# A gated attention stage: one projection step in every unit, maxima over eleven units, rank operations one at a time, masked products in other units

## The reference, cut to what matters

```python
ss = sigmoid(x @ Ws).reshape(b, t, H, E)          # H = 8 heads, E = 5 experts, DH = 64
sd = sigmoid(x @ Wd).reshape(b, t, H, E)
ms, md = topk_mask(ss, 3), topk_mask(sd, 3)       # the 3 best of 5 experts
q = einsum('bthed,bthe->bhtd', q5, sd * md)       # q5, k5, v5: x projected per head and expert
k = einsum('bthed,bthe->bhtd', k5, ss * ms)
v = einsum('bthed,bthe->bhtd', v5, ss * ms)
out = softmax(q k^T * DH**-0.5) v
y = einsum('bthem,bthe->btm', (out @ Wo).reshape(b, t, H, E, DIM), md)
```

## Time and profile before

| quantity | value |
|---|---|
| median of three runs | 4450.3 us |
| the profiled execution | 4442.77 us, span 4441.0 us |
| PE, DVE, POOL, ACT busy over the span | 87%, 73%, 66%, 43% |
| mean granted PE clock | 0.944 of full |
| gated stage | 1233.3 to 2619.7 us of the span |
| its pairs 0 to 13 | 1330.8 to 2459.4 us |
| pair 14, pair 15 with the ending | 60.7 us, 99.6 us |

### The profile page before, as it was taken

One profiled execution on the slowest core, in us unless ns is written; L12 is line 12 of the kernel. 1 busy time (PEld: TensorE's weight loads), 2 busy tenths in 40 slices (PEclk: granted clock), 3 DMA queues, 4 the chain that ended last, 5 costly groups with the idle time before them and its releaser, 6 DMA issues. The chain is left out here.

```text
span 4441.0 us, 63434 instructions
## 1 busy us (share of the span) xinstructions
PE 3881.5 (87%) x22554; PEld 2209.9 (50%) x22554; DVE 3243.7 (73%) x5656; ACT 1923.2 (43%) x3478; POOL 2937.1 (66%) x2164
## 2 busy tenths in 40 slices
PE   5998998999868889889899847999999999999964
PEld 3555555555445555555555423555455445545523
DVE  3786877868577787777876627888788788878826
ACT  1443443444345455455455312444344444434423
POOL 0776775757626777877887833777677677767740
PEclk6999999999979999999999957999999999999987
DMA  3000000000020000100000021122212221212111
GB/s 53 14 14 14 24 14 24 18 6 6 1 75 27 19 28 27 37 19 28 32 28 10 6 62 25 29 38 35 39 29 40 32 40 29 42 24 41 19 53 33
DMA packets 98041, 125.90 MB, mean 28 GB/s; under 512 B 28896, under 2 KB 76448, under 8 KB 97728
## 3 DMA queue, kind: packets, MB, share of 16 engines
q1 hardware_dynamic: 97728, 121.86, 12.5%
HBM read 103.69 MB, written 18.12 MB: 27 GB/s over the span
## 5 line engine op out<-in xcount | busy, mean ns | idle before, releaser
L776 POOL TENSOR_TENSOR s_psum_p<-s_psum_p,s_prob 128x1024 f32<-128x1024 f32 (+3 forms) x640 | 1335.6, 2087 | 388.3 <-ACT s_prob L511 338.3
L511 ACT ACTIVATE s_prob<-s_sT 128x1024 f32<-128x1024 f32 (+2 forms) x896 | 791.6, 931 | 877.2 <-DVE s_sT L658 495.1
L412 PE MATMUL s_pv<-s_prob,s_vp 128*64 128x512 f32 (+3 forms) x3584 | 797.7, 566 | 3.9 <-POOL s_prob L761 3.9
L614 DVE CUSTOM_DVE_ANT_0 s_mx<-s_mx,s_strip 128x512 f32<-128x512 f32 x640 | 429.6, 712 | 177.2 <-PE s_mx L371 174.7
L1670 POOL TENSOR_TENSOR s_psum_p<-s_psum_p,s_prob 128x1024 f32<-128x1024 f32 x192 | 462.1, 2407 | 104.7 <-ACT s_prob L1393 102.6
L1393 ACT ACTIVATE s_prob<-s_sT 128x1024 f32<-128x1024 f32 x256 | 262.4, 1025 | 581.9 <-PE s_sT L1257 581.9
L371 PE MATMUL s_mx<-s_bh,s_ah 64*128 64x512 f32 (+3 forms) x1792 | 412.1, 455 | 110.3 <-DVE s_bm L604 48.3
L663 DVE RECIPROCAL s_recip<-s_recip 128x128 f32<-128x128 f32 x512 | 452.4, 921 | 35.2 <-ACT s_recip L459 35.2
L776 POOL TENSOR_TENSOR s_psum_p<-s_prob 128x1024 f32<-128x1024 f32 (+1 forms) x128 | 288.0, 2250 | 236.2 <-ACT s_prob L511 233.5
L604 DVE TENSOR_REDUCE s_bm<-s_mx 128x8 f32<-128x1024 f32 (+3 forms) x384 | 367.4, 957 | 54.6 <-PE s_mx L371 45.7
L371 PEld LDWEIGHTS s_mx<-s_bh,s_ah 64*128 64x128 f32 x1792 | 171.9, 188 | 466.6 <-issue 192.1
(11 more groups left out here) (251 smaller groups left out, 7395.6 us busy)
## 6 DMA issues: line engine op xcount, KB each, us to landing
s_strip<-bias_rows SPq DMA_DIRECT2D x256, 144.0 KB, 5.7
s_wr<-gated_weights SPq DMA_DIRECT2D x32, 960.0 KB, 4.8
s_near<-bias_rows SPq DMA_DIRECT2D x256, 48.0 KB, 2.0
x<-s_x SPq DMA_DIRECT2D x12, 512.0 KB, 3.2
s_x<-x SPq DMA_DIRECT2D x8, 512.0 KB, 5.1
gated_weights<-s_side_hi SPq DMA_DIRECT2D x8, 480.0 KB, 2.6
gated_weights<-s_side_lo SPq DMA_DIRECT2D x8, 480.0 KB, 2.9
s_x<-in_L_attn_x_dram SPq DMA_DIRECT2D x4, 512.0 KB, 4.3
```

Source lines behind the costliest of these rows:

```text
L412: last = mm(pv[heads(hd), lo:CH], vp[:, g % 2, j, heads(hd)], prob[:, k % PR, hd, lo:CH], start=j == 0, stop=end)
L511: nc.scalar.activation(prob[:, k % PR, :, lo:CH], sT[:, k % 2, :, lo:CH], ACT.Exp, scale=st.scale).then_inc(exp_done, 1)
L614: last = nc.vector.tensor_tensor_reduce(out=mx[:, hd, :], in0=mx[:, hd, :], in1=strip[:, g % 2, hd, first:first + CH], scale=1.0, scalar=N ...
L776: nc.gpsimd.tensor_tensor(out[:, :, lo:CH], src, p[:, :, lo:CH], ALU.add)\
```

## The change

Only the gated stage's schedule and what follows from it. Projections: one in each of the 16 units, so that every one borrows. Maxima: one in units 4 to 9, two in 10 to 14. `mt` moves to unit 15 and, on PE and DVE, ahead of that unit's projection. Masked products of tokens 0 to 3 move to units 0 to 3 of the next pair; those of the last pair go to the head of `ending`. `gx` and `gl` move to units 12 to 15 of pairs 0, 3, 7; the ranks' sixteen operations become single jobs in units 0 to 9 of pairs 1, 4, 8. `xs` and `ln` are moved. Items take half 0 of queries and keys first, then half 1, and wait only for the projection steps that they read.

```diff
-TOPS, TOPC = E0 + 1, 8 + 3 * (E0 - 1)
+TOPS, TOPC = 4 + 3 * (E0 - 1), 8 + 3 * (E0 - 1)
...
-        self.mx_steps = [0] * 4 + [1] * 6 + [2, 2, 3, 3, 0, 0]
-        self.pj_steps = [2] * 4 + [1] * 8 + [0] * 4
+        self.mt_unit = 15
+        self.mx_steps = [0] * 4 + [1] * 6 + [2] * 5 + [0]
+        self.pj_steps = [1] * self.U
...
-            for i in range(4, NB):
-                out[3 + i].append(("zp", g - 1, i))
+            for i in range(NB):
+                out[i if i < 4 else 3 + i].append(("zp", g - 1, i))
...
-        for i in range(4):
-            out[12 + i].append(("zp", g, i))
...
-            for u, job in ((6, ("gx", gated, 0)), (7, ("gx", gated, 1)), (8, ("gl", gated, 0)),
-                           (9, ("gl", gated, 1)), (10, ("top", gated, 0)), (11, ("top", gated, 1)),
-                           (14, ("top", gated, 2))):
+            for u, job in ((12, ("gx", gated, 0)), (13, ("gx", gated, 1)), (14, ("gl", gated, 0)),
+                           (15, ("gl", gated, 1))):
...
-            for k, u in enumerate((8, 9, 11)):
-                out[u].append(("top", ranked, 3 + k))
+            for n, u in enumerate((0, 1, 2, 3, 4, 4, 5, 5, 6, 6, 7, 7, 7, 8, 9, 9)):
+                out[u].append(("top", ranked, n))
...
-        if p == 1 and b + 1 < B:
-            for k in range(2):
-                out[12 + k].append(("xs", b + 1, k))
-        for n, (of, u) in enumerate(((1, 13), (1, 14), (1, 15), (2, 2), (2, 3), (2, 6), (2, 7))):
+        if b + 1 < B and p in (1, 2):
+            out[13 if p == 1 else 0].append(("xs", b + 1, p - 1))
+        for n, (of, u) in enumerate(((1, 15), (1, 15), (2, 4), (2, 5), (2, 6), (2, 6), (2, 9))):
...
+        ending = [("zp", GP - 1, i) for i in range(4)] + ending
...
-                    pe.wait_ge(p_done, 2 * 2 * NB * (of + 1))
+                    pe.wait_ge(p_done, 2 * step(of, NB + 4 * (k // 2) + 4)[0])
...
+                if ("mt", g + 1) in todo:
+                    m_transpose(g + 1)
                 for n, t in enumerate(steps):
                     project(t[1], t[2], k if n == 0 else None)
...
-                if ("mt", g + 1) in todo:
-                    m_transpose(g + 1)
```

More of the change, by code:

```diff
@@ L1122, in misc_job @@
                 if kind == "item":
-                    pe.wait_ge(p_done, 2 * 2 * NB * (of + 1))
+                    pe.wait_ge(p_done, 2 * step(of, NB + 4 * (k // 2) + 4)[0])
                     for n in range(4):
                         last = nc.tensor.transpose(misc[:, n * P:(n + 1) * P],
-                                                   qkv[:, of % 3, 4 * (k % 2) + n, k // 2, :], cst.ident[:, :])
+                                                   qkv[:, of % 3, 4 * (k // 2) + n, k % 2, :], cst.ident[:, :])
                     last.then_inc(ab_full, 1)
@@ L1175, in project @@
                 m, hd, i = step(g, n)
-                if n == 0:
-                    pe.wait_ge(xl_done, 2 * (g // NP) + 2)
+                if n in (0, 4):
+                    pe.wait_ge(xl_done, 2 * (g // NP) + 1 + n // 4)
                 if n % NB == 0:
@@ L1324, in misc_job @@
                         act.wait_ge(st_full, (of - 1) * U)
-                    dst = ah if k < 2 else bh
-                    copy(dst[:, of % 2, half(k % 2)], misc[:, :]).then_inc(hi_done, 1)
+                    dst = bh if k % 2 else ah
+                    copy(dst[:, of % 2, half(k // 2)], misc[:, :]).then_inc(hi_done, 1)
                 elif kind == "gx":
@@ L1363, in x_hi @@
                 if b > 0:
-                    act.wait_ge(px_full, 2 * NB * NP * b)
+                    act.wait_ge(px_full, 2 * NB * NP * b - 4 * (1 - c))
                 copy(xh[:, half(c)], xT[:, half(c)]).then_inc(xh_done, 1)
@@ L1444, in misc_job @@
                 if kind == "item":
-                    hi, lo = (ah, al) if k < 2 else (bh, bl)
-                    cols = half(k % 2)
+                    hi, lo = (bh, bl) if k % 2 else (ah, al)
+                    cols = half(k // 2)
                     dve.wait_ge(hi_done, 4 * of + k + 1)
@@ L1512, in x_lo, with top_experts @@
                 tt(xl[:, half(c)], xT[:, half(c)], f32(xh[:, half(c)]), ALU.subtract).then_inc(xl_done, 1)
-            def top_experts(b, k):
+            def top_experts(b, n):
                 gates, kept = gate[:, b % 2, :, :], keep[:, :, :]
-                at = TOPC * b + E0 + 3 * (k - 1)
-                if k == 0:
+                k, part = divmod(n + 2, 3)
+                if n == 0:
                     dve.wait_ge(sig_done, 2 * b + 2)
@@ L1521, in top_experts @@
                         nc.vector.memset(kept[:, e, :], float(E0 - 1 - e)).then_inc(top_step, 1)
-                elif k < E0:
+                    return
+                dve.wait_ge(top_step, TOPC * b + E0 + n - 1)
+                if k < E0:
                     later, earlier, won = slice(k, E0), slice(0, E0 - k), beats[:, 0:E0 - k, :]
[L1524 to L1529, removed]
-                else:
[L1531 to L1535, removed]
+                    if part == 0:
+                        ins = tt(won, gates[:, earlier, :], gates[:, later, :], ALU.is_ge)
+                    elif part == 1:
+                        ins = tt(kept[:, later, :], kept[:, later, :], won, ALU.add)
+                    else:
+                        ins = tt(kept[:, earlier, :], kept[:, earlier, :], won, ALU.subtract)
+                elif part == 0:
+                    ins = nc.vector.tensor_scalar(kept, kept, float(TOP) - 0.5, None, ALU.is_lt)
+                elif part == 1:
+                    ins = tt(gates, gates, kept, ALU.mult)
+                else:
                     if b >= 2:
                         dve.wait_ge(share_done, 2 * NP * (b - 1))
-                    nc.vector.tensor_copy(
+                    ins = nc.vector.tensor_copy(
                         keep_d[:, b % 2, :, :, :],
-                        kept.rearrange("p e (i s h) -> p e i s h", i=NB, s=2)[:, :, :, 1, :])\
-                        .then_inc(top_step, 1)
+                        kept.rearrange("p e (i s h) -> p e i s h", i=NB, s=2)[:, :, :, 1, :])
+                ins.then_inc(top_step, 1)
+                if n == TOPS - 1:
                     dve.wait_ge(top_step, TOPC * (b + 1))
@@ L1624, in _ @@
                     maxima(t[1], t[2], second(todo, t, k))
+                if ("mt", g + 1) in todo:
+                    max_rows(g + 1)
                 for n, t in enumerate(steps):
@@ L1632, in _ @@
                             head_maxima(t[1])
-                    elif t[0] == "mt":
-                        max_rows(t[1])
                     elif t[0] == "ln":
```

## The result

The changed kernel takes 4466.4 us (median of six runs, 4462.3 to 4467.2) against 4449.8 for the kernel before in its six (4441.8 to 4451.1): ratio 1.0037, 95% interval [1.0025, 1.0049]. It is slower by 17 us, where the prediction has 4472 against 4450.3, slower by 22. The profiled execution has a span of 4460.7 us, 19.7 over that of before.

A forecast was written before the change was run, and what follows sets the result against it. PE bounds units 0 to 3, a chain through the borrowed half of sT units like 6, DVE the last four. Terms +52 +5 -24 -6 -3 +3 = +27 on 4442.8 give 4470, taken as 4472 us; range 4447 to 4503.

The forecast's parts named there:

- The chain through the borrowed half: Scores, projection, DVE scalings, scores, once a unit: units 0 to 3 -3.2 us, 12 to 15 +6.9; +52 over fourteen pairs.
- The upper bound: Upper limit of the cost in the changed units: 0.3 us more a unit for unseen waits, +4.9 a pair, +69.
- Masked products: Four products moved into units 0 to 3 meet POOL's additions: +5 us, bounds 0 and +24.
- The term of 0.6 in nine ordinary pairs: Only the worst meeting of product and addition, in unit 2, reaches the chain: +0.6 us a pair, +5 in all.
- The upper bound's 1.7 a pair: Upper limit for masked products: half a 4.28 us less DVE's spare time, in every pair, 14 x 1.7 = +24.
- Ranks: Groups cost about 39 us; single operations leave 5 in each of pairs 1, 4, 8: -24, bounds -36 and -10.
- Output projection: Its y and gt now lie in units with slack: 3 x (3.1 - 1.2) = -6 us.
- xs, ln: They move between units of about equal slack: -3 us, bounds -5 and +5.
- The end: Pair 14 and after: four masked products reach into pair 14, four more into the ending: +3 us, bounds -3 and +10.
- Rival A: A wash: same mechanism, borrowed waits cost less (+2.5 us a pair), ranks vanish into slack (-36): 4450; chance 0.18.
- B: Faster: the chain's wait disappears in units 0 to 3 and 12 to 15, PE bounds them, pairs 75.7: 4411; chance 0.10.
- C: Much slower: products and ranks meet POOL's additions in most units, ranks no cheaper: about +65 us, 4515; chance 0.12.

The follow-up runs named there:

- experiment 2: Changed kernel with projections, maxima, row transposition and masked products back where they were; ranks, gates, xs, ln and items stay changed: 4406.0 us, ratio 0.9903.
- experiment 3: Changed kernel with only the masked products of tokens 0 to 3 back in units 12 to 15 of their own pair: 4455.7 us, ratio 1.0019.
- experiment 4: Changed kernel with the single projection of units 0 to 3 put into tile mx, so nothing is borrowed there: 4453.0 us, ratio 1.0008.
- experiment 5: As experiment 4, and in units 4 to 9 maximum and projection change tiles (maximum borrows sT, projection in mx): 4420.8 us, ratio 0.9939.
- experiment 8: As experiment 6, and in units 4 to 9 maximum and projection change tiles: 4372.8 us, ratio 0.9835.
- experiment 9: As experiment 2, and in units 4 to 9 maximum and projection change tiles: 4371.3 us, ratio 0.9828.
- experiment 6: Kernel before with only the expert ranks changed, to sixteen single operations in units 0 to 9 of pairs 1, 4, 8: 4408.4 us, ratio 0.9913.
- experiment 10: As experiment 9, with one maximum less in units 10 and 11, two more in unit 14, row transposition heading unit 15: 4381.1 us, ratio 0.9844.

## Why the prediction was right

The direction, the size and the main step held, with two terms mis-sized that largely cancel; by its own steps:

- **The chain through the borrowed half.** Predicted: 18.4, 41.5 and 19.8 us for the three parts of the pair; measured 18.6, 41.3 and 19.8. Net 3.7 a pair and 52 in all; measured 3.7, and 48 to 53 from the steps alone (experiments 2 and 3). Unit 1 was worked out as 4.52 and took 4.55. That the wait is the cause and not a companion is shown by experiments 4, 5, 8 and 9, where only the tile was changed, for units 0 to 3 and 4 to 9. In units 12 to 15 it is seen (in pair 11 the scores start 0.09 to 0.11 after the last scaling), but no run takes it away there. The 3.7 aren't all idle time of PE: in pair 11 that rises by 2.2 and the busy time by 1.5, for the same 378 matmuls at a clock of 1.00; behind a wait single records are longer (scores of 0.43 to 0.44 for 0.40), and why is not shown. The upper bound has a slip: 0.3 more in each of the eight changed units is +6.1 a pair and not +4.9.
- **Masked products.** Predicted +5 in the pairs and +3 at the end; measured 7 by the medians and 10 by the stage (experiment 3 against the changed kernel). The size is right by luck, as it lies in another place. The term of 0.6 in nine ordinary pairs isn't there, since DVE's slack takes it. In unit 2 of pair 11 the product did take 2.40 us, held by an addition, as foreseen, and nothing waited for it. Where it decides is where a rank operation stands behind it: pairs 4 and 8, with 5.6 of the 6.0 us. (The upper bound's 1.7 a pair doesn't follow from its words: half of 4.28 less the microsecond to spare is 1.1.) Units 3 and 4 of pair 4, on DVE and PE (timeline):

```profile
1672.66 0.84 DVE L1478 TENSOR_TENSOR s_prod<-s_ztok,s_share 128x640 f32<-128x640 f32 x1
1673.42 2.88 DVE L1529 TENSOR_TENSOR s_keep<-s_keep,s_beats 128x512 f32<-128x512 f32 x1
1676.23 0.68 DVE L1448 TENSOR_TENSOR s_bl<-s_misc,s_bh 128x512 fp32r<-128x512 f32 x1
1676.96 0.66 PE L1146 MATMUL s_misc<-constants,s_z 128*128 128x128 f32 x4 [1.18 <-DVE s_bl L1448]
1679.50 2.25 DVE L1525 TENSOR_TENSOR s_beats<-s_gate 128x384 f32<-128x384 f32 x1
```

  The rank operation, 0.69 for its shape where nothing holds it, takes 2.88, the item's subtraction (L1448) comes late behind it, and PE, which needs `misc` free for the next transposes, waits 1.18. The next rank operation, 0.56 alone, takes 2.25 in the same way. That path, through the item and `misc` and not through the scalings, I hadn't named. With the products away (experiment 3) the same two rank operations take 0.91 and 0.55, and units 3 and 4 4.52 and 4.77 us instead of 5.44 and 6.83.
- **Ranks.** Predicted: groups cost 39, single operations 15. Measured 43.8 and, in the changed kernel, about 6.5 (pair 1 is 0.5 over pair 2, pairs 4 and 8 are 3.0 over pair 12). The gain was undersized, -24 for -37: this is the largest miss of the sum, partly offset by the next point. The stalls of up to 4 us in the earlier trace rows are gone, and with them the lower clock behind them, which the prediction never names though the earlier trace rows has it.
- **Output projection.** Predicted -6: wrong. Pair 12 is 2.9 over pair 11 where it was 3.1 over. Its six more matmuls, 2.93 us in unit 12, fill the slack of 0.8 and go beyond it (7.1 us for that unit), so nothing was gained.
- **xs, ln** were put at -3; experiments 2 and 6 differ by 0.1 in pairs 0 to 13. The end, +3: stage time from pair 14 on went from 153.8 to 155.0.
- **The sum** is +27; the medians moved by 17 and the two profiled executions by 19.5. The forecast of +22 came closer because 27 was added to a low execution (4442.8) and the result set near it: that much is luck.

Rival A had the cost right in kind and too small (2.5 a pair; it is 3.7), B falls by unit 1 (4.55, not 4.2 or less), C by the products' 7 to 10 us and the ranks' gain. Of rank stalls A was nearly right: they vanish almost entirely.

## What to carry to other kernels

A second piece of work in another buffer can be what hides the wait for the first; an even spread takes that cover away. Before spreading, list for each piece which buffer the next step waits for, and lend the buffer that is needed soonest to the piece that is read out soonest. Against that, short operations of an engine that has slack should be spread singly: in groups, 37 us were lost for the same work, about a third of them as longer busy time of PE, at the lower clock that followed its stalls.

## What the runs showed that I had not expected

The time before the stage. The profiled executions of the kernels before and after reach pair 0 at 1330.8 and 1330.6 us, the ten experiments at 1335.0 to 1336.4, but for two at 1333.5 and 1333.6, though the code up to there is the same but for the order of items. The profiled run of before took 4442.8 and its six runs lie between 4441.8 and 4451.1. So some 3 to 6 us of a single run's time are decided before the stage begins. The first two were not measured together with the ten, and which chip they ran on isn't recorded; but two experiments of one chip (2 and 5) are 2.9 apart as well. What decides it stays open, and comparisons of one run each at 0.1% are worth little here. Stage times therefore stand beside medians.

An operation of 0.82 us can cost 2.44 by where it begins: DVE's product waits for the rest of POOL's addition (experiment 10). The Trainium skill, "SBUF — State Buffer", section "Who interferes with whom", says of such a pair that the later one is blocked until the first ends; the rows agree, with 0.7 us of the product's own left after the end. That PE's schedule feels this only through what is queued behind on DVE is what the runs add.
